# A two-layer gated FFN in fp32: gate and up projections as Strassen's seven products

## The reference

```python
def lora_add(base, inp, A, B):                      # A, B: [batch's choice]
    t = einsum('bri,bni->bnr', A, inp)
    return base + einsum('bor,bnr->bno', B, t) * 0.5
gate = lora_add(x @ W_gate.T, x, A_gate, B_gate)    # 1376 features
up   = lora_add(x @ W_up.T,   x, A_up,   B_up)
act  = silu(gate) * up
y    = lora_add(act @ W_down.T, act, A_down, B_down)
nx   = y * rsqrt(mean(y*y) + 1e-5) * ln_w
out  = x + (silu(nx @ gate_w.T) * (nx @ up_w.T)) @ down_w.T   # 1792 features
```

## Time and profile before

| | |
|---|---|
| median of 3 runs | 450.1 us (450.0 to 451.2) |
| span of the profiled execution | 448.0 us, 6,658 instructions |
| TensorE (PE) busy | 442.1 us, 99%, 2,134 matmuls |
| VectorE (DVE) busy | 201.7 us, 45% |
| ScalarE (ACT) busy | 173.7 us, 39% |
| DMA | 29.11 MB, mean 65 GB/s |

### The profile page before, as it was taken

The page is one execution under the profiler, slowest core; times in us unless marked ns, Lnnn a source line. Parts: engine busy times, 40 slices in busy tenths (PEclk is TensorE's granted clock), DMA queues, the critical chain, the costliest instruction groups (busy, mean ns, idle before and its releaser), DMA issues.

```text
span 448.0 us, 6658 instructions
## 1 busy us (share of the span) xinstructions
PE 442.1 (99%) x2134; PEld 371.2 (83%) x2134; DVE 201.7 (45%) x447; ACT 173.7 (39%) x367; POOL 2.5 (1%) x12
## 2 busy tenths in 40 slices
PE   7999999999999999999999999999999999999997
PEld 5898888888888888888888888888888888888887
DVE  3899944444425366574452222222222351533510
ACT  5788533333324539363242222222222241422400
POOL 2000000000000000000000000000000000000000
PEclk9999999999999999999999999999999999999999
DMA  7672321123100001001041111121111000121111
GB/s 251 184 166 99 115 94 70 70 70 95 40 15 9 0 2 70 0 0 70 1 140 71 70 70 70 70 70 70 70 70 71 1 0 23 49 70 47 47 47 48
DMA packets 14146, 29.11 MB, mean 65 GB/s; under 512 B 1970, under 2 KB 4274, under 8 KB 14002
## 3 DMA queue, kind: packets, MB, share of 16 engines
q1 hardware_dynamic: 14130, 28.91, 19.6%
HBM read 26.81 MB, written 2.10 MB: 65 GB/s over the span
## 4 chain that ended last, share of the span: by engine, by line
PE 92%; DMA 3%; SPq 3%; DVE 1%; issue 1%; ACT 1%
PE bank L748 56%; PE bank L850 31%; PE bank L871 2%; PE bank L757 2%; DMA raw_gu<-wgu_in 2%; SPq L220 2%; DMA raw_d<-wd_in 1%; PE bank L859 1%; DVE pb L574 0%; SPq L206 0%; ACT wd L295 0%; DVE wd L497 0%; SPq L209 0%; ACT pb L340 0%; SPq L207 0%
## 5 line engine op out<-in xcount | busy, mean ns | idle before, releaser
L748 PE MATMUL bank<-xT,wgu 128*128 128x512 f32 (+1 forms) x1176 | 269.9, 386 | 1.6 <-DVE xT L497 1.6
L748 PEld LDWEIGHTS bank<-xT,wgu 128*128 128x128 f32 x1176 | 214.7, 188 | 44.7 <-issue 1.5
L850 PE MATMUL bank<-wd,pb 128*128 128x512 f32 (+1 forms) x642 | 143.8, 377 | 0.0
L850 PEld LDWEIGHTS bank<-wd,pb 128*128 128x128 f32 x642 | 112.5, 188 | 20.0 <-DVE pb L689 0.7
L333 ACT ACTIVATE silu<-bank 128x512 f32<-128x512 f32 x48 | 28.4, 594 | 110.8 <-PE bank L748 75.0
L538 DVE TENSOR_TENSOR act_f<-silu,bank 128x512 f32 (+1 forms) x28 | 19.3, 688 | 97.6 <-PE bank L748 96.3
L295 ACT ACTIVATE wgu<-raw_gu 128x512 fp32r<-128x512 f32 x48 | 27.8, 624 | 44.3 <-PE bank L748 23.8
L295 ACT ACTIVATE pb<-act_f 128x256 fp32r (+1 forms) x56 | 22.0, 415 | 42.7 <-PE bank L850 39.8
L538 DVE TENSOR_TENSOR act_c<-silu,bank 128x512 f32 (+1 forms) x20 | 13.7, 687 | 43.7 <-PE bank L757 43.7
L497 DVE TENSOR_TENSOR wgu<-raw_gu,wgu 128x512 fp32r<-128x512 f32 x48 | 31.0, 686 | 4.8 <-ACT wgu L295 4.4
L497 DVE TENSOR_TENSOR pb<-act_f,pb 128x256 fp32r<-128x256 f32 x56 | 22.7, 424 | 12.3 <-ACT pb L295 12.3
(11 more groups left out here) (61 smaller groups left out, 164.4 us busy)
## 6 DMA issues: line engine op xcount, KB each, us to landing
raw_gu<-wgu_in SPq DMA_DIRECT2D x24, 512.0 KB, 3.3
raw_d<-wd_in SPq DMA_DIRECT2D x25, 256.0 KB, 3.3
tok<-x_in SPq DMA_DIRECT2D x8, 256.0 KB, 2.5
out<-tok SPq DMA_DIRECT2D x7, 256.0 KB, 2.0
act_c<-xT_in SPq DMA_DIRECT2D x4, 256.0 KB, 4.1
act_c<-xT_in SPq DMA_DIRECT2D x2, 512.0 KB, 6.9
act_c<-bgu_in SPq DMA_DIRECT2D x8, 128.0 KB, 3.9
ad_raw<-ad_in SPq DMA_DIRECT2D x8, 88.0 KB, 2.4
```

The costliest lines, as they stand in the source:

```text
L748: ins = mm(bank[2 * chunk + g][:, lo:hi], wgu[:, par, g, s, k * P:(k + 1) * P], xT[:, r, k, chunk * CH + lo:chunk * CH + hi], start=(k == ...
L850: ins = mm(z[:, cols], pb_t[:, ft, s, t * P:(t + 1) * P], wd_t[:, ft, r, cols], start=(ft == 0 and s == 0 and r == 0), stop=(ft == last an ...
```

## The change

For two tiles of features (F1, F2), the two halves of the 512 input features (K1, K2) and the two halves of the tokens, a gate or up group is a 2 by 2 block product. It is now Strassen's form with seven block products (Winograd's variant) instead of eight. A block product is 2 blocks of input features by 3 passes, 6 matmuls. Three of the weight blocks and four sums of them, three of the x blocks and four sums of them are operands, each with a high and a low part. Sums of products are made in PSUM: q1 = W11 X11 is copied to a second bank and both go on; the product g and, after P6, the second bank are copied to SBUF and added by VectorE to later products.

Ten groups (`G1`) of the first layer and fourteen of the second follow each other with two banks of each sort, by parity. Names: `q1`, `g_prod`, `p4`, `p6`, `q2`, `p3`, `p7` are the block products; `ca`, `cm`, `cu` ScalarE's copies of q1, g and u2; `sums` VectorE's weight sums; `hi_a`/`lo_a` and `hi_b`/`lo_b` the parts of the weight blocks and of their sums; `c22_sum` the sum for block C22; T1 to T4 the sums of x blocks.

The A products have matmuls of their own (24 of 512 columns, all eight batches); a mask multiplies what does not belong to a batch by zero (`t_mask`), and `t_hi`, `t_lo` split the result. The B operand is put together in SBUF by 12 DMAs from SBUF to SBUF a group (`fill`) instead of by copies on the engines. Both down products have the weights stationary, so features are on partitions everywhere and there are no transposes; the down LoRA's second product has two matmuls a bank (`lora_c`); the mean square is a product with a matrix of ones (`sum_squares`, 16 matmuls), and square root, reciprocal and Newton's steps work on 512 columns. The output is stored feature by token, and the host turns it.

```diff
         @block.sync
+            def fill(buf, first, count):
...
+                for row, part in ((0, 0), (32, 1), (64, 0)):
+                    for q in range(4):
...
+                        sp.dma_start(v32(stack[row:row + 32, buf, q, :]).rearrange("p (i m) -> p i m", i=2), v32(piece)
+                                     ).then_inc(s_stk[buf], 16)
...
+            load_w(0)
+            for b in range(B):
...
+                sp.dma_start(agu_raw[:, b], agu_in[ds(which[b], 1)].rearrange(
+                    "o p (g k r) -> (o p) g k r", g=2, k=KT)).then_inc(s_agu_ld, 16)
+            load_w(1)
+            for b in range(B):
+                sp.dma_start(bgu_raw[RANK * b:RANK * b + RANK, :],
+                             bgu_in[ds(which[b], 1)].rearrange("o r m -> (o r) m")).then_inc(s_bgu_ld, 16)
+            sp.wait_ge(s_bgu_lo, 1)
+            fill(1, 0, 1)
+            fill(0, 0, 2)
+            load_w(2)
+            sp.wait_ge(s_shl, 2)
+            fill(1, 1, 2)
...
+            for n in range(2, 5):
+                load_wd(n)
+            sp.wait_ge(s_c22f, G1 // 2)
+            sp.wait_ge(s_c12f, G1 // 2)
+            for t in range(2):
+                for b in range(4):
+                    for row in (0, 64):
+                        sp.dma_start(bdr[row + RANK * b:row + RANK * b + RANK, t, :],
+                                     bd_in[ds(which[4 * t + b], 1)].rearrange("o r h -> (o r) h")
+                                     ).then_inc(s_bd_ld, 16)
+            for n in range(5, FC):
+                load_wd(n)
...
         @block.scalar
...
+            hi_a(0)
+            a.wait_ge(s_xsum[0], 1)
+            hi_x(0, XT1, xsum_c[:, 0])
+            hi_bgu(0)
+            hi_a(1)
+            t_hi(0)
+            hi_b(0)
+            t_neg()
+            ca(0)
+            t_hi(1)
+            short_silu(0)
+            short_silu(1)
+            ca(1)
+            for i, c in ((1, XT2), (2, XT3), (3, XT4)):
+                a.wait_ge(s_xsum[0], i + 1)
+                hi_x(0, c, xsum_c[:, i])
+            c11(0)
+            cm(0)
+            hi_b(1)
+            hi_bgu(1)
+            hi_bgu(2)
+            cu(0)
...
+            for m in range(4):
+                square(m)
+                if m == 0:
+                    hi_ac(20)
+            hi_ac(21)
+            rsqrt(0)
...
+            for m in range(4, 8):
+                square(m)
+            ca(G1)
+            ca(G1 + 1)
+            rsqrt(1)
+            nc.scalar.preload_act_table(ACT.Silu)
+            c11(G1)
+            for i, c, raw in ((0, XT1, xsum_f[:, 0]), (1, XT2, xsum_f[:, 1]), (0, X22, nx1[:, 2:4, :]),
+                              (2, XT3, xsum_f[:, 2]), (3, XT4, xsum_f[:, 3])):
+                a.wait_ge(s_xsum[1], i + 1)
+                hi_x(1, c, raw)
+                if c == XT1:
+                    cm(G1)
+            cu(G1)
+            hi_b(G1 + 1)
...
         @block.vector
...
+            lo_a(0)
+            def between(i):
+                if i == 0:
+                    lo_x(0, XC["t1"], xs[:, XT1, 1], xsum_c[:, 0], xs[:, XT1, 0])
+                    lo_bgu(0)
+                    lo_a(1)
+                    v.wait_ge(s_maskr, 1)
+                    t_mask(0)
+                    t_lo(0)
+                    sums(0)
+                    lo_b(0)
+                    t_mask(1)
+                    t_lo(1)
+                    short_act(0)
+                    short_act(1)
+                else:
+                    lo_x(0, XC[f"t{i + 1}"], xs[:, (XT1, XT2, XT3, XT4)[i], 1], xsum_c[:, i], xs[:, (XT1, XT2, XT3, XT4)[i], 0])
+            x_sums(0, xa0, xa1, xsum_c, between)
+            sums(1)
+            lo_b(1)
+            c11(1)
+            c12(0)
+            lo_bgu(1)
+            lo_bgu(2)
...
+            lo_wd(0)
+            lo_ac(0)
+            c22_sum(G1 - 1)
...
+            def norm(t):
...
+                v.wait_ge(s_rs, t + 1)
+                nc.vector.reciprocal(r, r).then_inc(s_nw, 1)
...
         @block.tensor
+            def q1(j):
+                pe.wait_ge(s_walo, j + 1)
...
+                elif j == 1:
+                    pe.wait_ge(s_tm, 8)
+                product(A_BANK[j % 2], j, W11, X11, True).then_inc(s_q1, 1)
...
+            def opening(j, ph, order, before_q2):
+                q1(j)
+                q1(j + 1)
+                before_q2()
+                q2(j)
+                q2(j + 1)
+                g_prod(j, ph, order["t1"])
+                p6(j, ph, order["t2"])
+                p3(j, ph, order["22"])
+                p7(j, ph, order["t3"])
+                g_prod(j + 1, ph, 0)
+                pe.wait_ge(s_xlo[ph], order["t4"])
+                p4(j)
+                p6(j + 1, ph, 0)
+                p3(j + 1, ph, 0)
+                p7(j + 1, ph, 0)
+            def group(j):
+                q1(j)
+                g_prod(j, 0, 0)
+                p4(j - 1)
+                p6(j, 0, 0)
+                q2(j)
+                p3(j, 0, 0)
+                p7(j, 0, 0)
```

More of the change, by code:

```diff
@@ new lines, in _, with group @@
+            x_sums(0, xa0, xa1, xsum_c, between)
+            sums(1)
+            lo_b(1)
+            c11(1)
+            c12(0)
+            lo_bgu(1)
+            lo_bgu(2)
+            def group(j, first, last):
+                if j % 2 == 1:
+                    c22_sum(j - 1)
+                else:
+                    c22_sum(j - 1)
+                    c22_act(j - 1)
+                if j + 1 < last:
+                    sums(j + 1)
+                if j % 2 == 0:
+                    c21(j - 1)
+                if j + 1 < last:
+                    lo_a(j + 1)
+                    lo_b(j + 1)
+                if j % 2 == 1 and j != first + 1:
+                    c11(j)
+                c12(j)
@@ new lines, in _, with ending @@
+            for j in range(1, G1):
+                group(j, 0, G1)
+                if j == 7:
+                    lo_ad()
+            def ending(j):
+                c22_sum(j)
+                c22_act(j)
+                c21(j)
+            lo_wd(0)
+            lo_ac(0)
+            c22_sum(G1 - 1)
+            c22_act(G1 - 1)
+            lo_wd(1)
+            lo_ac(1)
+            c21(G1 - 1)
+            for n in range(2, FC - 1):
+                lo_wd(n)
+                lo_ac(n)
+            lo_wd(FC - 1)
@@ new lines, in _ @@
+            lo_ac(10)
+            lo_bd()
+            for u in range(11, 19):
+                lo_ac(u)
+            td_sum(0)
+            td_lo(0)
+            lo_ac(19)
+            for m in range(4):
+                square_lo(m)
+                if m == 0:
+                    lo_ac(20)
+            lo_ac(21)
+            v.wait_ge(s_lnw, 16)
+            norm(0)
+            sums(G1)
+            lo_a(G1)
+            lo_b(G1)
+            for m in range(4):
+                scale(m)
+            v.wait_ge(s_nx, 4)
@@ new lines, in _ @@
+            x_sums(1, nx0, nx1, xsum_f, between_f)
+            sums(G1 + 1)
+            lo_b(G1 + 1)
+            c11(G1 + 1)
+            c12(G1)
+            group(G1 + 1, G1, G2)
+            lo_wd(FC)
+            for j in range(G1 + 2, G2):
+                group(j, G1, G2)
+                lo_wd(FC + j - G1 - 1)
+            lo_wd(FC + FF - 1)
+            lo_af(0)
+            c22_sum(G2 - 1)
+            c22_act(G2 - 1)
+            lo_af(1)
+            c21(G2 - 1)
+            for u in range(2, 2 * FF):
+                lo_af(u)
@@ new lines, in product, with lora @@
+                return ins
+            def lora(z, buf, cols, g, t, neg=False, alone=False):
+                t_op = tneg[0:KS, g, :] if neg else tgu[0:KS, t, g, :]
+                m = cols.stop - cols.start
+                for q in range(2):
+                    half = slice(256 * q, 256 * q + 256)
+                    ins = mm(z[0:m, half], stack[0:KS, buf, 2 * t + q, cols], t_op[:, half],
+                             start=(alone and q == 0), stop=(q == 1), skip_group_check=True)
+                return ins
@@ L929, in _ @@
[L929 to L937 removed]
+                    ins = mm(T_BANK[t][:, :], ad[0:rows, n, t, :], slot_c(u, r)[0:rows, :],
+                             start=(first and r == 0), stop=(last and r == 1), skip_group_check=True)
@@ new lines, in _ @@
+            rest(0)
+            rest(1)
+            pe.wait_ge(s_tdhi, 4)
+            pe.wait_ge(s_tdlo, 2)
+            close(0)
+            close(1)
+            rest(2)
+            close(2)
+            pe.wait_ge(s_ev, 4)
+            sum_squares(4)
+            sum_squares(5)
+            rest(3)
+            close(3)
+            sum_squares(6)
+            sum_squares(7)
+            opening(G1, 1, XF, lambda: None)
+            for j in range(G1 + 2, G2):
+                group(j)
```

1568 lines of the change are left out of this document (853 added, 715 removed).

## The result

The changed kernel takes **504.99 us** (median of four, 504.2 to 506.57) against 450.05: a ratio of 1.1227, 95% interval 1.1201 to 1.1253. The forecast was slower, at 489, with a range up to 503: the side was right, the time 16 us more than forecast and 2 us outside the range. The profiled execution took 504.2 us, its span 502.5.

The account below looks back on a forecast made before the run. TensorE was taken as the bound: 422.2 us without holes, plus 56.4 of holes, 7.0 for reciprocals and 2.0 for the clock, gave 487.6 profiled, 489 as a run; own range 470 to 500, with rivals 466 to 503.

Parts of the forecast that it names:

- The distance: ... I take 0.2285: All TensorE work: products of 512 columns follow each other 0.2285 us apart, read from the old kernel's trace.
- The steady groups are covered.: Loops: a second-layer group's 9.6 us of TensorE covers VectorE's 7.2 and ScalarE's 5.5, every wait met.
- The rival of VectorE as the bound: Loops: VectorE takes 10.5 us a second-layer group instead of 7.2, 12.6 us more, 502 in all; chance 0.10.
- The rival of the low clock in the openings: Both openings: the clock stays low behind the holes, 6 us above forecast, 495 in all; chance 0.15.
- The holes made by order: Openings, between layers, loop end: TensorE waits for work queued in order on other engines; all holes sum to 56.4 us.
- The clock ... I take 2.0; ends: 0, and 8: Second opening: restarting after idling costs 2.0 us of slow products; 8 if some 40 products run at 0.43.
- the td hole: Between the layers, before the second td chain (down LoRA's inner product) is met: TensorE idles 1.1 plus 3.5 us.
- 1,756 x 0.2285: Whole kernel: 1,756 products of 512 columns at one distance, with 88 x 0.12, make 411.8 us.
- products 0.43 apart at the full clock: Sign of being wrong in the new profile: granted clock at full while products stand 0.43 us apart.
- I take 25: First opening: the B matrices, loaded whole, land at 25 us; 26 at 181 GB/s, 23 at 250.
- The 12 stack fills there, at 0.46 us an issue: First layer's groups: 12 fills take 5.5 us to issue, then 1.7 to land, within 13 us available.
- The reciprocal, 4.2: Reciprocal on 512 columns takes 4.2 us, ends 0.69 and 5.3; twice on the path, adding 7.0 us.

Follow-up runs that it names:

- experiment 9: Six dummy products of 512 columns added to each of the 20 loop groups of the changed kernel; 534.56 us, ratio 1.1852.
- experiment 1: Changed kernel with hi_ac(20) and lo_ac(20) moved from between the first and second square to behind the fourth; 501.71 us, ratio 1.1126.
- experiment 2: Changed kernel with the second half's td chain moved ahead of the scalings and parts of the next layer's input; 497.04 us, ratio 1.1012.
- experiment 7: Changed kernel with only the second opening reordered: square root ahead of q1's copies, cm(10), cu(10) later, group 11's sums early; 493.65 us, ratio 1.0969.
- experiment 4: Changed kernel with 142 dummy products in TensorE's long waits of both openings and ahead of the td chain; 498.72 us, ratio 1.1072.
- experiment 5: Changed kernel with every down-stage product given 128 rows, the surplus rows zero; 500.3 us, ratio 1.1096.
- experiment 10: Changed kernel with squares, td chain, both openings reordered, 128 rows, fills on two queues, B's second part before fills, c22_sum(9), c22_sum(23) earlier; 461.84 us, ratio 1.0283.
- experiment 3: Changed kernel with the reciprocal of 512 columns left out, a multiplication by 1 in its place; 495.45 us, ratio 1.0987.

## Why the forecast was right in its side and short in its size

One sum first: 487.6 and 2.1 are 489.7, not 489; the forecast was 15 us short by its own terms.

- *"The distance: ... I take 0.2285", and the product count.* Right: 1,856 matmuls; in the stretch from the second opening to the end the forecast of 198.5 us was met by 198.6. "26 us under the old one ... all the change can bring" is borne out by experiment 9.
- *"The steady groups are covered."* Right, by experiment 9 and by the unbroken stretches from 300 us on. The rival of VectorE as the bound (502 us) lies nearer to the measured time than the forecast does, and its mechanism is not there: the time alone would have confirmed the wrong story. The rival of the low clock in the openings (495) had the right cause, but its largest piece lay between the layers.
- *The holes made by order.* Right in place, the large ones within 1 us of their size except q1(1)'s (15.53 for 12.1) and the stack's (5.68 for 4), the late ones of both openings too large; experiments 1, 2 and 7 undid or shortened them. The squares' 4.9 measured 4.1, of which 1.9 was hi_ac(20)'s.
- *"The clock ... I take 2.0; ends: 0, and 8".* This is the step that failed most. Measured: 6.3 us by experiment 4, net of what it lost elsewhere; 4.6 lie in one place to which the forecast gave nothing, the products behind the td hole, and 3.4 in the second opening, where it had its 2.0. It had counted restarts in the two openings alone, while a hole of 4.19 us, which stood in its own list as 4.6, was enough, and smaller ones at times (below). The rule of the Trainium skill ("TensorE: Matmul & The Clock Gate", why this matters for your kernels), that idle gaps between bursts bring back half the clock, agrees with these rows: 12 products in 5.28 us behind the gap, 3.03 without it. Here it should have outweighed the silence of a trace that had no long gap.
- *"1,756 x 0.2285": every product at one price.* It failed for the heads, at the product of 64 rows: 3.4 us by the rows, within the 4.7 of experiment 5, which also holds clock. The forecast had named products 0.43 apart at the full clock as a sign of being wrong; at the heads they are 0.42 apart. The old trace could not have priced them: it has products of 96 rows, at the usual distance, and none of 64.
- *"I take 25" for B, and "The 12 stack fills there, at 0.46 us an issue".* Both too low: 29.0 and 0.60 to 0.68. B had been reckoned from 181 GB/s and more; from 15 to 29 us the changed kernel moved 146. The fills had been priced by loads from HBM, whereas they go from SBUF to SBUF, with 32 partitions each. Together 5.3 us at the end of the opening, the later waits being partly hidden under them.
- *The reciprocal, 4.2.* Too high by 0.85 each time, which took 1.7 us off the sum in the other direction.

Of the 15.7 us in the table, the clock behind the td hole is 4.6, B and the fills with the slow products of that opening 5.3, the heads 3.4, the reciprocal -1.7. The rest, 4.1, is spread: 0.6 in the first loop, some 2 around the sums of squares, where products are slow too, and 1.6 in the second opening, where slow products outweigh the smaller holes. Hand-overs between engines, which the forecast had left out at 3 us, may be in it; that was not shown. Its own range of 470 to 500 added up ends of 6, 2 and 3 upwards and had no end for a product at another price.

## What to carry to other kernels

A change that saves products on a TensorE-bound kernel is worth those products only as long as its extra sums and copies stay off the path; list the holes that it makes, and charge each for its length and, as an upper end, for the slow products that may follow: up to 4.6 us behind one hole here, nothing behind others. When a stage waits at a late point, look for the bound behind the first one before pricing the fix: here two edits gave nothing alone and, with B's loads moved, 15.5 us together. And a product of a shape that the old trace does not hold has no price yet: give it a range.

## What had not been expected of the hardware

- Five products in a row with 96, 96, 96, 128 and 64 rows took 1.56 us; the same five with 128 rows 1.13. The 0.4 more lie at the product of 64 rows: 0.33 us before it, 0.42 behind it. Products of 96 rows that followed 128 rows kept 0.228.
- A DMA issue from SBUF to SBUF (32 KB, 32 partitions) took SyncE 0.60 us as the median, 0.68 in a row of 24 and 0.79 in a row of 36; GpSimd issued 12 in 6.29 us, 0.52 each. The old kernel's loads of L206 and L244 took 0.46 and 0.50. Landing took 1.9 and 1.8 us.
- How long products stay slow behind a wait is not fixed by the wait. Behind the td hole (4.18 to 4.26 us in three kernels) twelve products took 5.28 us in the changed kernel, 4.42 in experiment 1 and 3.02 in experiment 5. Behind waits of 1.5 and 0.75 us twelve took 4.50 in experiment 1 and 2.90 in experiment 10; behind one of 2.11 (experiment 10) 4.51; undisturbed 2.88 to 3.02. One hole of 1.24 us (experiment 3) left the next products at full rate. After one of 8.01 (experiment 7) 30 products took 9.78 us, 2.9 more than at 0.2285.
- The reciprocal of 512 columns took 3.352 us, 6.5 ns a column; of one column 0.164.
